# Sorting edges while a transformer runs: three tiles counted at once, in four parts of the edges, at two fixed places of a group

## The chip, the core and the metric

The kernel runs on one core of a Trainium2 chip. A core has a matrix engine (TensorE, PE in the rows; PEld is its weight load), a vector engine (VectorE, DVE), a scalar engine (ScalarE, ACT), a general-purpose engine (GpSimd, POOL) and a queue engine (SyncE, SP). Each runs its own instruction stream, and they wait for each other by semaphores. SP, ACT and POOL issue DMAs. The time is the device time of one launch in microseconds (us), lower is better; before and after are compared by the median of several runs.

## The reference

There are 6250 nodes with 256 features, and 100,000 edges with a source, a destination and a weight. Cut to what matters:

```python
xn = layernorm(x)
# gnn: edge attention, 4 heads of 64
feats = einsum('nd,hdo->hno', xn, Ws) + bs
a_s, a_d = feats . aw_src, feats . aw_dst
w = exp(-relu((a_s[src] + a_d[dst] + aw_e * edge_weight + ab) / 20))
gnn = segment_sum(w * feats[dst], src) / segment_sum(w, src)
# mix: 4 layers, 8 heads of 32, linear attention over all nodes
for l in range(4):
    h = layernorm(y) * g1 + b1
    q = softmax(h Wq * s, over a head's 32 columns)
    k = softmax(h Wk * s, over the 6250 nodes)
    y = y + (q (k^T (h Wv))) Wo + bo
    y = y + gelu((layernorm(y) * g2 + b2) W1 + c1) W2 + c2
x1 = x + gnn + mix
# ffn: 8 heads of 64 slices, attention among slices, weights over all nodes
x1 = x1 + slice_attention(layernorm(x1))
```

The edges come in no order of their source, so the sum over a node's edges needs them sorted by tiles of 125 source nodes.

## The kernel before, in words

The nodes are 50 tiles of 125 rows, and four tiles make a group: 13 groups, 0 to 12, the last with two tiles. All matrix work is fp32.

**One list orders all engines.** A planner writes `stages`, a list of steps with an assumed duration each: `x_t` (transpose the input rows), `feats` (edge features), `h1_t`, `keys`, `queries`, `q_exp`, `q_sum`, `q_norm`, `q_t` (the queries' softmax and its transpose), `ek_t`, `context` (transposed exponentials of the keys, and their product with h), `attend`, `h2_t`, `up`, `down` (the feed-forward half). Every engine walks the same list and issues its own share of each step, so the list is the program order of all of them. Three kinds of other work are laid into it at planned times, from a second list, `beside`, and a third, `blocks`:

- **The sort** (`sort`, L1069 and on), wholly on DVE. The edges lie as 125 rows of 800 columns. Steps 1 to 4 make each edge's tile number. Steps 5 to 29 (`FIRST_COUNT` on) count two tiles each: a match against the pair's number (L1101), a running sum along the row in which the odd tile has a weight of 2^10 (L1102), the row's total (L1103), the match times the sum (L1104), added to `rank` (L1105). One step is five instructions. Step 30 unpacks the two fields, and step 33 (`COUNT_STEP`) turns the totals into offsets with two matmuls of PE. Then four parts of 200 columns follow, 13 steps each; one of these steps looks up the offset of four tiles for the part (L1143 and L1144 for each tile). When a part is done, POOL scatters its 200 columns as records of 12 bytes to DRAM, one indirect DMA a column (L806), 800 in all.
- **The load of the sorted records** (`edges` on SP, `records` on DVE, `rows` on PE), at a planned time after the first part: 1.55 us for each column.
- **The edge blocks**, 220, spread evenly over the feed-forward groups from the records to the end of the last layer. For each, POOL gathers 4 x 128 rows of `gather_table` with four indirect DMAs (L772); DVE makes one-hot matrices, scores and weighted rows and adds the result into `acc` (L1158 to L1174, L1412); PE sums with twelve matmuls (L1746, L1757). A gather may run six blocks ahead, since it has a ring of six buffers.

**The first pass** is the stretch in which `x_t` and `feats` of group s stand beside layer 0's `context` of group s - 2 and `keys` and `queries` of group s - 1. Its sort steps stand 12 us of the plan apart, wherever that falls. After it come the last groups of a layer (`last_groups`, `finish`) and then the feed-forward groups of layer 0, which also hold the keys and queries of layer 1, and so on for four layers. The slice attention of `ffn` ends the kernel.

## Time and profile before

| | |
|---|---|
| runs | 3549.72, 3547.07, 3549.95 us; median 3549.72 |
| the profiled execution | 3542.55 us, its span 3540.8 us |
| busy in the span | PE 93%, DVE 66%, POOL 56%, ACT 34% |
| mean granted TensorE clock | 0.968 of 2.4 GHz |
| first pass | to 323 us |
| scatter of the records (L806) | 530 to 1788 us |
| gathers (L772) | 1811 to 3088 us |

All stretches below are microseconds from the span's start. Busy shares are averages over stages whose limits differ: PE is full where nothing else is laid in, and has gaps in the first pass, in the feed-forward groups that hold the sort, and in those that hold the edge blocks. The mean clock is below 1 where PE has had gaps.

### The profile page before, as it was taken

To read this page: it belongs to the slowest core of one execution; us is meant where nothing else is said; L and a number is where in the kernel's file an instruction comes from. 1 tells how busy PE (TensorE), PEld (TensorE's weight loads), DVE (VectorE), ACT (ScalarE), POOL (GpSimd) and SP (SyncE) were. 2 spreads that over 40 slices of the span, in tenths; PEclk is the share of its full clock that TensorE was granted. 3 is DMA by queue.
4 is the path that set the end of the run, shared out by engine and by line. 5 is a ranking of instruction groups with operands and counts; after the bars stand their busy time and mean duration, and the time that the engine had idled before them with its cause. 6 is when DMAs were issued, how large, how long until landed. Compare 5 with 4: busy or idle time off the path is not lost.

```text
span 3540.8 us, 43968 instructions
## 1 busy us (share of the span) xinstructions
PE 3280.0 (93%) x13948; PEld 2325.2 (66%) x13948; DVE 2344.0 (66%) x6105; ACT 1188.5 (34%) x2126; POOL 1981.9 (56%) x1746
## 2 busy tenths in 40 slices
PE   6887899999989999989999989988999999989989
PEld 4565566666756666766766666666766666655666
DVE  7887878885444444453468777776776767759941
ACT  3343232333333333333324433343433434312220
POOL 3210007777777777777746777774777777600000
PEclk9998999999999999999999999999999999999999
DMA  3332112222322222232234555554555555412124
GB/s 114 105 99 87 32 45 43 43 49 38 75 52 45 46 49 49 43 85 42 48 107 134 148 141 143 137 149 147 154 161 150 159 142 168 130 52 87 67 108 152
DMA packets 226436, 338.52 MB, mean 96 GB/s; under 512 B 52502, under 2 KB 180009, under 8 KB 225956
## 3 DMA queue, kind: packets, MB, share of 16 engines
q0 software_dynamic: 67840, 119.33, 15.7%
q1 hardware_dynamic: 120452, 161.93, 14.1%
q10 hardware_dynamic: 37920, 54.45, 4.8%
q8 instruction: 119, 1.95, 0.2%
q14 instruction: 105, 0.86, 0.1%
HBM read 247.40 MB, written 87.29 MB: 95 GB/s over the span
## 4 chain that ended last, share of the span: by engine, by line
PE 61%; DVE 13%; POOL 13%; issue 5%; DMA 4%; ACT 2%; DVEq 0%; ACTq 0%
PE bank_v L1715 14%; PE bank_a L1700 14%; POOL arena L772 13%; PE bank_e L1757 5%; PE bank_a L1617 4%; PE bank_v L1645 3%; PE bank_v L1605 3%; PE bank_v L1688 3%; PE bank_a L1546 3%; PE bank_v L1776 3%; DMA arena<-gather_table,arena 3%; PE bank_v L1866 3%; PE bank_v L1788 2%; PE bank_a L1628 1%; DVE acc L1102 1%
## 5 line engine op out<-in xcount | busy, mean ns | idle before, releaser
L806 POOL DMA_INDIRECT edge_records<-acc x800 | 962.7, 1203 | 535.3 <-issue 535.3
L772 POOL DMA_INDIRECT arena<-gather_table,arena x880 | 943.9, 1073 | 356.5 <-issue 260.2
L1715 PE MATMUL bank_v<-W_sb,gT 128*125 128x256 f32 x3200 | 746.7, 385 | 0.0
L1700 PE MATMUL bank_a<-hT,W_sb 128*128 128x500 f32 (+1 forms) x1664 | 716.6, 579 | 17.2 <-ACT gT L832 8.6
L1715 PEld LDWEIGHTS bank_v<-W_sb,gT 128*125 128x125 f32 x3200 | 592.3, 190 | 106.3 <-issue 23.2
L1700 PEld LDWEIGHTS bank_a<-hT,W_sb 128*128 128x128 f32 x1664 | 319.4, 195 | 327.6 <-issue 301.3
L1757 PE MATMUL bank_e<-arena 128*125 128x260 f32 x1760 | 454.9, 403 | 0.0
L832 ACT ACTIVATE gT<-bank_a,cols 128x500 f32<-128x500 f32 (+1 forms) x416 | 272.3, 661 | 377.4 <-PE bank_a L1700 376.5
L1757 PEld LDWEIGHTS bank_e<-arena 128*125 128x125 f32 x1760 | 322.1, 193 | 46.7 <-issue 1.4
L832 ACT ACTIVATE hT<-bank_a,cols 128x500 f32<-128x500 f32 (+1 forms) x208 | 144.9, 747 | 489.5 <-PE bank_a L1546 460.4
L1158 DVE TENSOR_TENSOR arena<-arena 128x1024 f32<-128x1024 f32 x220 | 268.2, 1219 | 0.0
L1351 DVE TENSOR_TENSOR xs<-bank_v,xs 125x512 f32<-125x512 f32 x100 | 68.8, 688 | 261.5 <-PE bank_v L1715 261.3
L966 ACT ACTIVATE esc<-esc 128x16 f32<-128x16 f32 x220 | 47.1, 214 | 554.9 <-DVE esc L1174 554.5
L1412 DVE TENSOR_TENSOR acc<-acc,bank_e 125x260 f32 x440 | 184.5, 419 | 65.0 <-PE bank_e L1757 44.7
L1263 DVE TENSOR_REDUCE kst<-bank_a 128x1 f32<-128x500 f32 (+1 forms) x104 | 67.1, 656 | 233.5 <-PE bank_a L1617 232.9
L1645 PE MATMUL bank_v<-h,ek 125*128 125x256 f32 x800 | 185.8, 385 | 3.1 <-ACT ek L832 3.1
L766 POOL TENSOR_SCALAR xs<-xs,st_x 125x256 f32<-125x256 f32 x50 | 68.7, 1383 | 213.2 <-DVE st_x L1042 213.2
L1617 PE MATMUL bank_a<-hT,Wqkv 128*128 128x500 f32 (+1 forms) x416 | 179.8, 574 | 8.9 <-ACT hT L832 8.9
L1605 PE MATMUL bank_v<-Wqkv,hT 128*125 128x256 f32 x800 | 183.8, 382 | 0.0
L1605 PEld LDWEIGHTS bank_v<-Wqkv,hT 128*125 128x125 f32 x800 | 151.7, 190 | 38.5 <-issue 17.7
L1645 PEld LDWEIGHTS bank_v<-h,ek 125*128 125x128 f32 x800 | 152.9, 193 | 25.7 <-DVE gT L1283 2.8
L832 ACT ACT_TABLE_LOAD x126 | 161.7, 1283 | 10.9 <-issue 5.0
(286 smaller groups left out, 4342.4 us busy)
## 6 DMA issues: line engine op xcount, KB each, us to landing
residual<-xs SPq DMA_DIRECT2D x60, 500.0 KB
xs<-residual SPq DMA_DIRECT2D x60, 500.0 KB
arena<-edge_rows ACTq DMA_DIRECT2D x220, 125.0 KB
queries<-qT_out SPq DMA_DIRECT2D x48, 500.0 KB
qT_in<-queries ACTq DMA_DIRECT2D x39, 500.0 KB
arena<-gather_table,arena POOLq DMA_INDIRECT x880, 3.7
edge_records<-acc POOLq DMA_INDIRECT x800
slice_weights<-arena SPq DMA_DIRECT2D x12, 1000.0 KB, 5.0
```

The costliest lines, as they stand in the source:

```text
L772: e.indirect_dma_start(g_of(j)[:, i, :], None, table_d, bass.IndirectOffsetOnAxis(ap=node[:, TE * j + i:TE * j + i + 1].bitcast(I32), axis ...
L806: e.indirect_dma_start(rec_d, bass.IndirectOffsetOnAxis(ap=pos_i[:, f:f + 1], axis=0), r3[:, f, :], None).then_inc(d_rec, 16)
L832: e.activation(to, of, func, **k).then_inc(a_done, 1)
L1158: e.tensor_tensor(gf, gf, bc(g[:, :, HG * DG:ROW].unsqueeze(3), [P, TE, HG, DG]), ALU.mult)\
L1412: e.tensor_tensor(to, to, ps_sum[h], ALU.add).then_inc(e_done[h], 1)
L1546: o = e.transpose(b[:, i * R:(i + 1) * R], X[:, i, c * P:(c + 1) * P], ident[0:R, 0:R])
L1605: o = e.matmul(b[0:R, i % 2 * D:(i % 2 + 1) * D], hv[:, k, i * R:(i + 1) * R], W[:, k, 0:D], start=k == 0, stop=k == KC - 1)
L1617: o = e.matmul(b[:, 0:n], W[:, k, D + c * P:D + (c + 1) * P], hv[:, k, 0:n], start=k == 0, stop=k == KC - 1)
L1645: o = e.matmul(b[:, c * D:(c + 1) * D], ek[:, a:a + P], h1[:, i * D:(i + 1) * D], start=i == 0, stop=i == tiles(s) - 1)
L1700: o = e.matmul(b[:, 0:n], W[:, k, f * P:(f + 1) * P], hv[:, k, 0:n], start=k == 0, stop=k == KC - 1)
L1715: o = e.matmul(b[0:R, i % 2 * D:(i % 2 + 1) * D], gv[:, f, i * R:(i + 1) * R], W2_sb[:, f * D:(f + 1) * D], start=False, stop=f == FB - 1 ...
L1757: o = e.matmul(ps_sum[h], oh_ring[j % NO][:, i * R:(i + 1) * R], g_of(j)[:, i, :], start=i == TH * h, stop=i == TH * (h + 1) - 1)
```

## The change

The sort counts three tiles in one step. A tile's number b is split into b // 3 and b % 3; the three kinds weigh 1, 256 and 65536 in the running sum. For a field to hold below 256, the sum starts anew in each of the four parts of 200 columns, so L1102 becomes four instructions over 200 columns in place of one over 800, and the totals are four columns a step. There are 17 such steps (4 to 20) in place of 25. Three steps (21 to 23) then unpack a field each, in place of one step, and step 23 adds the four parts' totals. `COUNT_STEP` is 25 in place of 33, and its offsets are made for each part (three more small additions). The preparation is rewritten (steps 1 to 3). The parts' 52 steps are as they were, but use their own part's offsets.

The plan changes too. In each group of the first pass the sort has two fixed places: after `context`, and between `queries` and `feats`. `feats` now stands in front of the queries' `q_exp`, `q_sum` and `q_norm`, and `q_t` moves from before `context` to after `h1_t`. After the first pass the rules are as before. Since there are eight steps fewer of 8 us, everything planned from the end of the first part moves: `edges` from 1651.65 to 1563.64 us of the plan, from the middle of group 4's `down` steps in layer 2 to group 2's, and the 220 blocks are spread over some two groups more: 3.35 us of the plan apart in place of 2.97, which is 13 or 14 blocks in a group of layer 2 in place of 15 or 16, and 9 or 10 in a group of layer 3 in place of 10 or 11.

```diff
-    FIRST_COUNT = 5
-    COUNT_STEP = FIRST_COUNT + NT // 2 + 3
+    FIRST_COUNT, NTRIO = 4, -(-NT // 3)
+    COUNT_STEP = FIRST_COUNT + NTRIO + 4
...
+    slots = []
     for s in range(2, NGR):
         put(1.05, "x_t", s)
         turn("ek_t", 0, s - 2)
+        context(0, s - 2)
+        slots.append(now())
+        turn("h1_t", 0, s - 1)
         turn("q_t", 0, s - 2)
-        context(0, s - 2)
-        turn("h1_t", 0, s - 1)
         keys(0, s - 1)
         if s <= PRE:
             queries(0, s - 1)
+        slots.append(now())
+        put(1.15 * tiles(s), "feats", s)
+        if s <= PRE:
             put(0.0, "q_exp", 0, s - 1)
             put(0.0, "q_sum", 0, s - 1)
             put(0.0, "q_norm", 0, s - 1)
-        put(1.15 * tiles(s), "feats", s)
...
     for k in range(SORT_STEPS):
+        if 1 <= k <= len(slots):
+            at = slots[k - 1] - 0.01
         beside.append((at, ("sort", k)))
-        at += 7.0 if k < FIRST_COUNT - 1 else 12.0 if at < mixed else 8.0 if k < COUNT_STEP else 4.5 if k < first_part else 7.0
+        at += 8.0 if k < COUNT_STEP else 4.5 if k < first_part else 7.0
...
-                elif FIRST_COUNT <= k < FIRST_COUNT + NPAIR:
+                elif FIRST_COUNT <= k < FIRST_COUNT + NTRIO:
                     b = k - FIRST_COUNT
-                    step(e.scalar_tensor_tensor(oh, pair, float(b), weight, ALU.is_equal, ALU.mult))
-                    step(e.tensor_tensor_scan(cum, oh, oh, 0.0, ALU.add, ALU.bypass))
-                    e.tensor_copy(cnt2[:, b:b + 1], cum[:, EC - 1:EC])
-                    step(e.scalar_tensor_tensor(oh, pair, float(b), cum, ALU.is_equal, ALU.mult))
+                    step(e.scalar_tensor_tensor(oh, trio, float(b), weight, ALU.is_equal, ALU.mult))
+                    for q in range(PARTS):
+                        o = e.tensor_tensor_scan(by_part(cum)[:, q, :], by_part(oh)[:, q, :], by_part(oh)[:, q, :], 0.0,
+                                                 ALU.add, ALU.bypass)
+                    step(o)
+                    e.tensor_copy(cnt3.rearrange("p (q b) -> p q b", q=PARTS)[:, :, b], by_part(cum)[:, :, PART - 1])
+                    step(e.scalar_tensor_tensor(oh, trio, float(b), cum, ALU.is_equal, ALU.mult))
                     step(e.tensor_tensor(rank, rank, oh, ALU.add))
...
+                elif FIRST_COUNT + NTRIO <= k < FIRST_COUNT + NTRIO + 3:
+                    m = k - FIRST_COUNT - NTRIO
+                    c3 = cnts.rearrange("p (q b k) -> p q b k", q=PARTS, k=3)[:, :, :, m]
+                    ci = trios[:, 0:PARTS * NTRIO]
+                    if m == 0:
+                        step(e.tensor_copy(pos_i, rank))
+                    step(e.tensor_copy(ci, cnt3))
+                    for a in (field, pos_i), (ci, ci):
+                        o = e.tensor_scalar(*a, 8 * m, 255, ALU.logical_shift_right, ALU.bitwise_and)
+                    step(o)
+                    e.tensor_copy(c3, ci.rearrange("p (q b) -> p q b", q=PARTS))
+                    if m == 0:
+                        step(e.scalar_tensor_tensor(rank, mod, 0.0, field, ALU.is_equal, ALU.mult))
+                    else:
+                        step(e.scalar_tensor_tensor(oh, mod, float(m), field, ALU.is_equal, ALU.mult))
+                        step(e.tensor_tensor(rank, rank, oh, ALU.add))
...
                     for b in range(4 * at, min(4 * at + 4, NT)):
-                        step(e.tensor_scalar(oh[:, h], bucket[:, h], float(b), adj[:, b:b + 1], ALU.is_equal, ALU.mult))
+                        step(e.tensor_scalar(oh[:, h], bucket[:, h], float(b), adj[:, part * NT + b:part * NT + b + 1],
+                                             ALU.is_equal, ALU.mult))
```

**On ACT, one group of the first pass, before** (`hT` with `cols` is `h1_t`, the other `hT` is `x_t`; `ekT` the keys' exponentials; L907 is `q_exp`; `h` and `gT` are `feats`):

```order
L832 ACTIVATE qT_out<-bank_a 128x500 x2
L832 ACTIVATE hT<-bank_a,cols 128x500 x2
L913 ACTIVATE kst<-kst 128x2
L832 ACTIVATE ekT,kst<-bank_a,kst 128x500 x2
L907 ACTIVATE qn<-qn 125x1024
L879 ACTIVATE h_1<-xs,st_x 125x256 x4
L832 ACTIVATE gT<-bank_a 125x264 x4
```

The same place after (L842, L889, L917 and L923 are those lines now):

```order
L842 ACTIVATE hT<-bank_a,cols 128x500 x2
L842 ACTIVATE qT_out<-bank_a 128x500 x2
L923 ACTIVATE kst<-kst 128x2
L842 ACTIVATE ekT,kst<-bank_a,kst 128x500 x2
L889 ACTIVATE h_1<-xs,st_x 125x256 x4
L842 ACTIVATE gT<-bank_a 125x264 x4
L917 ACTIVATE qn<-qn 125x1024
```

`q_exp`, which waits for DVE, has moved behind the features' evictions, and the eviction of `q_t` behind that of `h1_t`.

**On DVE, layer 1's queries of group 2, in a feed-forward group, before** (L1283 ends `queries`, L1335 is `attend`, L1292 and L1293 are `q_sum`, L1298 is `q_norm`; L1143 and L1144 are a sort step):

```order
L1292 TENSOR_REDUCE qst<-qn 125x32
L1293 RECIPROCAL qst<-qst 125x32
L1143 TENSOR_SCALAR acc<-acc 125x200
L1144 TENSOR_TENSOR acc<-acc 125x200
L1143 TENSOR_SCALAR acc<-acc 125x200
L1144 TENSOR_TENSOR acc<-acc 125x200
L1143 TENSOR_SCALAR acc<-acc 125x200
L1144 TENSOR_TENSOR acc<-acc 125x200
L1143 TENSOR_SCALAR acc<-acc 125x200
L1144 TENSOR_TENSOR acc<-acc 125x200
L1335 TENSOR_TENSOR xs<-bank_v,xs 125x512
L1298 TENSOR_TENSOR qn<-qn,qst 125x1024
```

The same queries after (L1308 and L1309, L1361, L1318, L1319, L1324; the sort step's lines are L1168 and L1170):

```order
L1309 TENSOR_TENSOR qn<-bank_v,qst 125x512
L1168 TENSOR_SCALAR acc<-acc 125x200
L1170 TENSOR_TENSOR acc<-acc 125x200
L1168 TENSOR_SCALAR acc<-acc 125x200
L1170 TENSOR_TENSOR acc<-acc 125x200
L1168 TENSOR_SCALAR acc<-acc 125x200
L1170 TENSOR_TENSOR acc<-acc 125x200
L1168 TENSOR_SCALAR acc<-acc 125x200
L1170 TENSOR_TENSOR acc<-acc 125x200
L1361 TENSOR_TENSOR xs<-bank_v,xs 125x512
L1318 TENSOR_REDUCE qst<-qn 125x32
L1319 RECIPROCAL qst<-qst 125x32
```

A sort step that stood between `q_sum` and `q_norm` now stands between `queries` and `q_sum`; in other groups the steps fall elsewhere.

**On PE, one edge block and what is around it in a group of layer 2, before** (L1746 and L1757 are the block's matmuls, L1761 its next row numbers; L1617 is `keys`, L1605 `queries`):

```order
L1617 MATMUL bank_a<-hT,Wqkv 128x500 x2
L1746 ISA
L1746 MATMUL bank_e<-as,arena 128x12 x2
L1746 ISA
L1746 MATMUL bank_e<-as,arena 128x12 x2
L1757 MATMUL bank_e<-arena 125x260 x4
L1761 TENSOR_LOAD tids
L1761 ISA x2
L1761 TENSOR_LOAD tids
L1761 ISA x2
L1617 MATMUL bank_a<-hT,Wqkv 128x500 x2
L1605 MATMUL bank_v<-Wqkv,hT 125x256 x4
```

And after (L1772, L1783, L1787; `keys` is L1643, `queries` L1631):

```order
L1643 MATMUL bank_a<-hT,Wqkv 128x500 x4
L1772 ISA
L1772 MATMUL bank_e<-as,arena 128x12 x2
L1772 ISA
L1772 MATMUL bank_e<-as,arena 128x12 x2
L1783 MATMUL bank_e<-arena 125x260 x4
L1787 TENSOR_LOAD tids
L1787 ISA x2
L1787 TENSOR_LOAD tids
L1787 ISA x2
L1631 MATMUL bank_v<-Wqkv,hT 125x256 x8
```

A block costs the same; more of the layer's own matmuls stand between two of them.

## Rows read from the trace of the kernel before

**Rows 1.** The page: busy time, then tenths busy in 40 slices.

```profile
PE 3280.0 (93%) x13948; PEld 2325.2 (66%) x13948; DVE 2344.0 (66%) x6105; ACT 1188.5 (34%) x2126; POOL 1981.9 (56%) x1746
...
DVE  7887878885444444453468777776776767759941
...
POOL 3210007777777777777746777774777777600000
PEclk9998999999999999999999999999999999999999
```

**Rows 2.** The page: the chain that ended last, by line.

```profile
PE bank_v L1715 14%; PE bank_a L1700 14%; POOL arena L772 13%; PE bank_e L1757 5%; PE bank_a L1617 4%; PE bank_v L1645 3%; PE bank_v L1605 3%; PE bank_v L1688 3%; PE bank_a L1546 3%; PE bank_v L1776 3%; DMA arena<-gather_table,arena 3%; PE bank_v L1866 3%; PE bank_v L1788 2%; PE bank_a L1628 1%; DVE acc L1102 1%
```

**Rows 3.** Groups by line, POOL, 1880 to 2380: busy, mean ns | idle before.

```profile
L772 POOL DMA_INDIRECT arena<-gather_table,arena x360 | 390.7, 1085 | 109.7 <-issue 107.5 <-PE bank_e L1757 2.1
```

**Rows 4.** The same, 2500 to 3080.

```profile
L772 POOL DMA_INDIRECT arena<-gather_table,arena x422 | 451.4, 1070 | 128.6 <-issue 125.2 <-PE bank_e L1757 3.4
```

**Rows 5.** Line L772: ns min/median/max, first and last start; who waited for it.

```profile
L772 POOL DMA_INDIRECT arena<-gather_table,arena x880: 940/946/2005, 1810.7 to 3087.1; - x176
...
  DVE esc L1174: 165.4, 84
```

**Rows 6.** Windows: us, then PE, PEld, DVE, ACT, POOL busy, granted clock, DMA.

```profile
106.85:304.98 198.13, 170.48 (x738) 122.74 (x737) 166.09 (x375) 80.65 (x176) 41.93 (x31) 0.91 0.29 93
...
431.91:875.89 443.98, 422.93 (x1679) 295.65 (x1678) 348.69 (x1027) 139.46 (x217) 263.71 (x220) 0.98 0.20 43
483.99:536.86 52.87, 48.49 (x187) 34.11 (x188) 46.76 (x145) 15.55 (x24) 5.45 (x5) 0.94 0.13 39
588.32:634.39 46.07, 45.88 (x187) 32.02 (x186) 41.63 (x122) 15.44 (x25) 35.14 (x30) 1.00 0.22 47
830.22:875.89 45.67, 45.67 (x187) 32.10 (x186) 21.67 (x65) 15.45 (x25) 34.72 (x30) 1.00 0.21 42
1900.00:2330.00 430.00, 396.81 (x1876) 291.60 (x1874) 338.33 (x875) 164.78 (x321) 335.99 (x309) 0.97 0.53 143
2490.00:3080.00 590.00, 555.28 (x2522) 399.25 (x2522) 414.71 (x1030) 237.93 (x416) 459.13 (x429) 0.98 0.55 154
```

**Rows 7.** Groups by line, DVE, 106.85 to 304.98: the counting steps.

```profile
L1102 DVE TENSOR_TENSOR_SCAN acc<-acc 125x800 f32<-125x800 f32 x14 | 27.2, 1944 | 0.5
L1101 DVE SCALAR_TENSOR_TENSOR acc<-acc 125x800 f32<-125x800 f32 x14 | 14.6, 1044 | 0.0
L1105 DVE TENSOR_TENSOR acc<-acc 125x800 f32<-125x800 f32 x14 | 14.4, 1026 | 0.5
L1104 DVE SCALAR_TENSOR_TENSOR acc<-acc 125x800 f32<-125x800 f32 x14 | 14.3, 1022 | 0.0
```

**Rows 8.** The same, DVE, 466 to 560: an instruction over 200 columns.

```profile
L1144 DVE TENSOR_TENSOR acc<-acc 125x200 f32<-125x200 f32 x65 | 23.9, 368 | 2.2
```

**Rows 9.** Pieces of the chain that ended last, after the first pass.

```profile
342.45 0.91 DVE acc L1101
```

**Rows 10.** Waits of PE, 431.91 to 875.89: us in total, times, longest.

```profile
PE bank_a L1546 <- DVE qn L1298: 19.1, 8, 4.4
```

**Rows 11.** Line L806, the scatter: ns min/median/max, first and last start.

```profile
L806 POOL DMA_INDIRECT edge_records<-acc x800: 1182/1187/2182, 530.2 to 1786.4; - x160
```

**Rows 12.** Timeline of SP, 1785 to 1792: start us, us.

```profile
1788.72 0.34 SPq L657 DMA_DIRECT2D queries<-qT_out  x1
1789.12 0.42 SPq L671 DMA_DIRECT2D arena<-edge_records  x1
```

**Rows 13.** Timeline of POOL, from 1865, and from 2415.

```profile
1871.05 0.97 POOL L772 DMA_INDIRECT arena<-gather_table,arena  x1 [18.62 <-PE bank_e L1757]
...
2451.68 0.94 POOL L772 DMA_INDIRECT arena<-gather_table,arena  x1 [35.30 <-PE bank_e L1757]
```

**Rows 14.** Timeline of PE, 1867 to 1875: a block and what follows.

```profile
1868.67 0.25 PE L1746 MATMUL bank_e<-as,arena 128*128 x4
...
1870.61 3.52 PE L1700 MATMUL bank_a<-hT,W_sb 128*128 128x500 f32 x8
```

87 lines of the change are left out of this document (41 added, 46 removed).

## The prediction, as put down before the run

> **What bounds the kernel now.** I read the page first. PE is busy for 93% of the span, and the rows of tenths say where it is not: DVE is nearly full in the first ten slices, POOL sits at a flat 7 tenths from slice 21 to 35, and PE's granted clock is 0.9 in the first four slices [rows 1]. The chain that ended last is mostly PE, but its third line is a POOL line, the gather L772, with 13% of the span [rows 2]. So I asked POOL's groups by line for the stretches with edge blocks. From 1880 to 2380, 360 gathers took 390.7 us and stood 109.7 us idle, 107.5 of it issue and only 2.1 waiting for PE: POOL does nothing but start one gather after another, one each 1.390 us [rows 3]. From 2500 to 3080 it is one each 1.374 us, 3.4 us of waiting in 580 [rows 4]. Seven tenths is POOL full. DVE waited for gathers 84 times, 165.4 us in all [rows 5]. In the same stretches PE lacks 33 of 430 us and 35 of 590, at clocks of 0.97 and 0.98 [rows 6]. I conclude that from about 1871 to 3088 POOL sets the pace, not PE, by its 880 gathers. When they may begin then matters more than what the sort costs.
>
> Earlier, the limits differ. In the first pass a group takes 198.13 / 8 = 24.77 us and DVE is busy for 84% of it. In the feed-forward groups that hold sort steps PE is the engine and loses time in single blows: a group without sort is 45.67 us, one that holds it well 46.07, one that holds it badly 52.87 at a clock of 0.94 [rows 6]. The blow is PE waiting for `q_norm`, 8 times for 19.1 us [rows 10].
>
> **Term 1, the first pass.** In the eight groups 4 to 11 DVE is busy for 166.09 us [rows 6]. 14 counting steps are in them, 27.2 + 14.6 + 14.4 + 14.3 = 70.5 us, 5.04 a step [rows 7]. The rest is 95.6 us, 11.9 a group, and idle time is 32.0 us, 4.0 a group. Now every group holds two counting steps. No row shows a scan over 200 columns. An instruction over 200 columns takes 368 ns and its like over 800 takes 1026 [rows 7, 8], which leaves a fixed part of (4 x 368 - 1026) / 3 = 149 ns. Four scans for one cost nothing more at best, if the fixed parts overlap (they have no wait between them), and 3 x 149 = 0.45 us more at worst. I take 0.35, near the upper end, since the nearest row is at it. A step is then 5.39 us, two 10.8, a group 22.7 us if DVE never idles and 26.7 if all of today's idle time stays. With `feats` in front of `q_exp`, ACT no longer makes PE's features wait for DVE's queries, and `q_norm` has a group's length until `q_t`; what should stay of the 4.0 us are the short gaps between dependent instructions, so I take 24.0. Eight groups give 8 x (24.0 - 24.77) = -6 us, between -16 and +16. PE then waits some 3 us a group for the keys' exponentials behind the first sort step: late next is ACT's `ekT`, released by DVE. The last group of the pass holds two unpacking steps in place of one counting step; it has no input statistics and no queries, so I put it at 0.
>
> **Term 2, between the first pass and the feed-forward.** Three counting steps stood there, of which the one that begins at 342.45 is on the chain that ended last [rows 9]. In their places stand now the third unpacking step (two instructions over 800 columns at about 1.03, one on integers no dearer, and some seven small ones: 3.9 us against 5.0) and an empty step (0 against 5.0). The step after them and the next are traded for `COUNT_STEP` and two lookups of eight 200-wide instructions, 8 x 0.37 = 2.9 us each, which I call even within 3 us. Sum -6 us.
>
> **Term 3, the sort in the feed-forward groups.** From 431.91 to 875.89 there are nine groups, 443.98 us [rows 6]. By the program's order five of them have a sort step between `q_sum` and `q_norm`, or the long unpacking step in front of `q_sum`; three have steps only where `q_exp` or the keys cover them; one has none. With 45.67 and 46.2 for the latter kinds the five come to (443.98 - 45.67 - 138.6) / 5 = 51.9 each, which is the 52.87 of the row. After, steps 46 and 66 fall between `q_sum` and `q_norm`, four groups have covered steps and three are empty: 2 x 51.9 + 4 x 46.2 + 3 x 45.67 = 425.6, so -18 us, between -8 (four blows) and -24 (one). What DVE saves in busy time, about 40 us, is not counted again: it is what these three terms are made of. Terms 1 to 3 are -30 us up to 876.
>
> **Term 4, the edges.** Today SP issues the load of the records at 1789.12, 0.4 us after the store of `queries` in front of it in the list [rows 12], and the last scatter starts at 1786.4 [rows 11]: place and readiness coincide. The place moves two feed-forward groups forward, 2 x 45.67 = 91, and with the 30 us comes at 1788.7 - 121 = 1668. Readiness: the first part now ends with step 38, in front of DVE's keys of the group whose `ek_t` is at 431.91 today; those begin some 8 us before it, so with 12 us gained and the step's own 3 the scatter starts near 415 in place of 530.2, and at today's length of 1256 us ends near 1672. SP waits about 5 us. Behind it on SP stands only the store of a group that DVE finishes later; behind that wait on DVE are the records' copies, some 20 us on. The first gather starts at 1810.7 today and near 1695 then. The ring of six first fills, and POOL is full from the fifth block on: 1871.05 today [rows 13], then 1871 - 91 + 8 (the block stands four and a half `up` steps further on, 1.76 each [rows 14]) - 30 = 1758. From there to the last gather it is 3087.1 - 1871 = 1216 us [rows 5, 13], the 35.3 us at the change of layers included; the gathers are the same, so the end comes 113 us earlier. Is PE in time? It lacked 68 us of 1020, and the clock's 0.97 and 0.98 cost 13 + 12, in all some 105 over 1216; the layer work that now lies within adds 83. PE needs 1216 - 105 + 83 = 1194 us. By the group of layer 2: 45.67 + 13.6 blocks x 1.94 [rows 14] = 72.1 for PE, 13.6 x 4 x 1.39 = 75.6 for POOL, in place of 76 and 87. Both are near full, so I take off 5 us for rubbing: -108 at the end of the blocks. Terms 1 to 3 are inside this, since they move the start. The rest of the kernel, from 3101 on, is the same work.
>
> A gather's median is 946 ns and its mean 1085 or 1070 [rows 3 to 5], so something stretches some of them. By the Trainium skill (SBUF — State Buffer, Who interferes with whom), copies and tensor_scalars of VectorE in a two-port mode hold a port pair shared with GpSimd, and the other engine is blocked for the whole instruction. If all the stretching came from the layer's own DVE work, 15.6 x 4 x 0.139 = 8.7 us a group would fall on 13.6 blocks: 0.02 us more a gather, 18 us in all, and the time would be 3460; if it came from the blocks' work, nothing.
>
> **Sum.** The profiled execution is 3542.55 us, its span 3540.8; 108 less is 3434.5. The runs' median is 3549.72, 7 us above it, and the time is compared with that: 3549.7 - 108 = 3442.
>
> **The rivals.**
> - *The first pass keeps its idle time.* A counting step after `context` meets POOL's normalisation, PE waits, its clock falls, and a group takes 27 us: 8 x (27 - 24.0) = +24, which moves the end one for one: 3466. For it: 26.7 is the bound above, and the clock there is 0.91 [rows 6]. Against it: PE has 3 us of slack a group. 14%.
> - *The blocks' losses are not POOL's.* If PE's gaps stay with the blocks for another reason, spreading them gives nothing, and only terms 1 to 3 remain: 3520. Against it: the 2.1 and 3.4 us of POOL's waits [rows 3, 4]. 8%.
> - *Slower: the edge stretch costs by the group, not by the block.* If a group of layer 2 with 13.6 blocks takes the 87 us that one with 15.6 takes, two more groups cost 2 x (87 - 45.67) = +83, less 30: 3602. It decides if DVE, 79% busy there (338.33 of 430 [rows 6]), sets the group rather than POOL. Against it: with two blocks fewer DVE has less to do. 4%.
> - *It doesn't start earlier.* If the scatter ends where it does today, the records wait for it, POOL's 1216 us begin at 1871 as now, and all of terms 1 to 3 is waited away: 3550. Against it: nothing stands between the first part and the scatter but a semaphore. 4%.
>
> **How the numbers follow.** The forecast, 3442, has 70%; its own range is 3424 to 3465. The range for 8 in 10 takes in the first rival and the ends of the unknown prices: 3415 to 3488; left out are the other rivals and a little of each tail. This kernel's measurement can tell about 0.2%, 7 us. Faster by more than that: 70 + 14 + 8 = 92%; within it 3% and slower 5%, from the last two.
>
> **What would show it.** The gather's first start near 1695 and its last near 2975, still one each 1.37 to 1.40 us with almost no wait for PE. The scatter's first start near 415, last near 1671. The windows of groups 4 to 11 at 24 us with DVE over 93% busy, and PE waiting for `ekT`. Waits of PE for `q_norm` in the feed-forward groups down from five of 3 to 4 us to two. Scans of 200 columns that start 0.43 to 0.59 us apart. The forecast is wrong if gathers wait for PE in long stretches (then PE is the bound), or if the first start of L772 has not moved by over 100 us.

## The result and the profile after

The changed kernel takes 3428.99 us, median of 4 runs (3426.59 to 3436.74), against 3549.10 (3547.07 to 3549.95; one run more than in the table above) of the kernel before on the same chip: ratio 0.9666, 95% interval 0.9649 to 0.9683, 120 us faster. The forecast was 3442. The profiled execution took 3427.19 us with a span of 3425.4. Lines of the code moved with the change: the gather is now L782 (was L772), the scatter L816 (was L806), the queries' softmax L1324 (was L1298).

The page, as [rows 1], and the chain that ended last, as [rows 2]:

```profile
PE 3236.0 (94%) x13948; PEld 2296.2 (67%) x13948; DVE 2302.2 (67%) x6124; ACT 1182.8 (35%) x2124; POOL 1980.3 (58%) x1746
...
DVE  7898888854544444544578878887677667659941
...
POOL 3210177777777777777557777775777777400000
PEclk9999999999999999999999999999999999989999
...
PE bank_a L1726 16%; PE bank_v L1741 15%; POOL arena L782 14%; PE bank_e L1783 6%; PE bank_a L1643 3%; PE bank_v L1671 3%; PE bank_v L1631 3%; PE bank_v L1802 3%; PE bank_v L1714 3%; PE bank_a L1572 3%; PE bank_v L1892 3%; PE bank_v L1814 2%; DVE acc L1110 1%; ACT arena L842 1%; DMA arena<-gather_table,arena 1%
```

POOL's row, idle for three slices behind the first pass before, is at 0 for one and at 1 for the next: the scatter starts sooner. At its far end the gathers stop in the same slice as before, which is 122 us earlier, since a slice is 85.6 us here and was 88.5. They are still on the chain, with 14%.

Windows (us, busy of PE, PEld, DVE, ACT, POOL, granted clock, DMA), as [rows 6]: first-pass groups 4 to 11; nine feed-forward groups; one with step 46 in front of `q_norm`; one with covered steps; one with step 66 in front of `q_norm`; one without sort; then two stretches of edge blocks.

```profile
109.29:296.19 186.90, 162.07 (x737) 114.71 (x737) 177.69 (x432) 78.51 (x176) 39.47 (x31) 0.99 0.31 99
411.97:836.95 424.98, 415.42 (x1676) 290.47 (x1674) 306.64 (x898) 139.25 (x217) 327.05 (x271) 0.99 0.22 45
458.52:507.63 49.11, 46.12 (x187) 32.08 (x186) 40.99 (x119) 15.53 (x25) 37.43 (x32) 1.00 0.23 44
554.10:600.71 46.61, 45.88 (x188) 32.00 (x186) 39.01 (x117) 15.38 (x24) 33.96 (x29) 1.00 0.22 46
600.71:653.40 52.69, 48.77 (x188) 34.20 (x187) 41.93 (x118) 15.64 (x25) 42.04 (x35) 0.94 0.21 41
791.28:836.95 45.67, 45.67 (x188) 32.09 (x186) 21.46 (x65) 15.46 (x25) 35.69 (x30) 1.00 0.21 42
1790.00:2200.00 410.00, 398.10 (x1905) 294.53 (x1905) 333.64 (x879) 172.37 (x324) 320.10 (x296) 0.99 0.54 148
2370.00:2960.00 590.00, 572.99 (x2628) 413.68 (x2627) 418.90 (x1060) 248.55 (x430) 432.86 (x404) 1.00 0.54 154
```

A first-pass group now takes 186.90 / 8 = 23.36 us with DVE busy for 95%. The nine feed-forward groups take 424.98, 19 less. In the edge stretch PE lacks 12 of 410 and 17 of 590, where it lacked 33 of 430 and 35 of 590.

The counting steps of the first pass by line, as [rows 7] (the sum is now four of 200 columns):

```profile
L1110 DVE TENSOR_TENSOR_SCAN acc<-acc 125x200 f32<-125x200 f32 x63 | 34.0, 599 | 0.6
L1108 DVE SCALAR_TENSOR_TENSOR acc<-acc 125x800 f32<-125x800 f32 x16 | 17.0, 1060 | 0.0
L1115 DVE TENSOR_TENSOR acc<-acc 125x800 f32<-125x800 f32 x15 | 14.9, 991 | 0.5
L1114 DVE SCALAR_TENSOR_TENSOR acc<-acc 125x800 f32<-125x800 f32 x15 | 14.7, 983 | 0.0
```

The gathers by line, 1760 to 2260 (answers to [rows 3]) and 2380 to 2960 (to [rows 4]):

```profile
L782 POOL DMA_INDIRECT arena<-gather_table,arena x361 | 389.5, 1079 | 111.6 <-issue 107.3 <-PE bank_e L1783 4.3
...
L782 POOL DMA_INDIRECT arena<-gather_table,arena x403 | 432.6, 1073 | 157.1 <-issue 118.1 <-PE bank_e L1783 39.0
```

The gather's line as a whole, with its first and last start and who waited for it (to [rows 5]), then the scatter's (to [rows 11]):

```profile
L782 POOL DMA_INDIRECT arena<-gather_table,arena x880: 940/947/2003, 1682.6 to 2965.3; - x176
...
  DVE esc L1200: 82.0, 48
```

```profile
L816 POOL DMA_INDIRECT edge_records<-acc x800: 1182/1187/2215, 408.7 to 1667.2; - x160
```

A gather each 1.388 us in the first window, as before. Of the 39.0 us of waiting in the second, 31.8 are the change of layers, which lies in it. DVE's own wait for gathers has halved.

The timelines of POOL (as [rows 13]) and of SP (as [rows 12]):

```profile
1750.22 0.94 POOL L782 DMA_INDIRECT arena<-gather_table,arena  x1 [26.87 <-PE bank_e L1783]
...
2402.05 0.94 POOL L782 DMA_INDIRECT arena<-gather_table,arena  x1 [31.80 <-PE bank_e L1783]
```

```profile
1660.53 0.35 SPq L667 DMA_DIRECT2D queries<-qT_out  x1
1670.70 0.34 SPq L681 DMA_DIRECT2D arena<-edge_records  x1
```

The fifth block, from which POOL is full, resumes at 1750.22 in place of 1871.05. From there to the last gather it is 2965.3 - 1750.2 = 1215.1 us, against 1216.

### The profile page after: what moved, and what is told of

It is laid out like the page before. It is cut to its first block, busy times and chain, and to the rows that moved or that the text cites. A ratio compares the mean times of both kernels' runs of the same rounds, so it can differ in the third digit from the quotient of the medians.

```text
span 3425.4 us, 43999 instructions
## 1 busy us (share of the span) xinstructions
PE 3236.0 (94%) x13948; PEld 2296.2 (67%) x13948; DVE 2302.2 (67%) x6124; ACT 1182.8 (35%) x2124; POOL 1980.3 (58%) x1746
## 4 chain that ended last, share of the span: by engine, by line
PE 64%; POOL 14%; DVE 12%; issue 5%; DMA 2%; ACT 2%; DVEq 0%; ACTq 0%
PE bank_a L1726 16%; PE bank_v L1741 15%; POOL arena L782 14%; PE bank_e L1783 6%; PE bank_a L1643 3%; PE bank_v L1671 3%; PE bank_v L1631 3%; PE bank_v L1802 3%; PE bank_v L1714 3%; PE bank_a L1572 3%; PE bank_v L1892 3%; PE bank_v L1814 2%; DVE acc L1110 1%; ACT arena L842 1%; DMA arena<-gather_table,arena 1%
## 5 line engine op out<-in xcount | busy, mean ns | idle before, releaser
L816 POOL DMA_INDIRECT edge_records<-acc x800 | 963.5, 1204 | 419.8 <-issue 419.8
L782 POOL DMA_INDIRECT arena<-gather_table,arena x880 | 942.4, 1071 | 355.6 <-issue 259.2
L1783 PE MATMUL bank_e<-arena 128*125 128x260 f32 x1760 | 442.0, 394 | 0.0
L842 ACT ACTIVATE gT<-bank_a,cols 128x500 f32<-128x500 f32 (+1 forms) x416 | 273.3, 661 | 408.9 <-PE bank_a L1726 408.0
L1783 PEld LDWEIGHTS bank_e<-arena 128*125 128x125 f32 x1760 | 314.4, 188 | 43.6 <-issue 1.4
L842 ACT ACTIVATE hT<-bank_a,cols 128x500 f32<-128x500 f32 (+1 forms) x208 | 144.9, 747 | 485.5 <-PE bank_a L1572 468.3
L1184 DVE TENSOR_TENSOR arena<-arena 128x1024 f32<-128x1024 f32 x220 | 267.9, 1218 | 0.0
L1643 PE MATMUL bank_a<-hT,Wqkv 128*128 128x500 f32 (+1 forms) x416 | 180.2, 574 | 6.2 <-ACT qT_out L842 4.0
L1631 PE MATMUL bank_v<-Wqkv,hT 128*125 128x256 f32 x800 | 181.9, 379 | 0.0
L1631 PEld LDWEIGHTS bank_v<-Wqkv,hT 128*125 128x125 f32 x800 | 150.0, 188 | 38.8 <-issue 18.5
```

The source lines that it names most:

```text
L782: e.indirect_dma_start(g_of(j)[:, i, :], None, table_d, bass.IndirectOffsetOnAxis(ap=node[:, TE * j + i:TE * j + i + 1].bitcast(I32), axis ...
L816: e.indirect_dma_start(rec_d, bass.IndirectOffsetOnAxis(ap=pos_i[:, f:f + 1], axis=0), r3[:, f, :], None).then_inc(d_rec, 16)
L842: e.activation(to, of, func, **k).then_inc(a_done, 1)
L1184: e.tensor_tensor(gf, gf, bc(g[:, :, HG * DG:ROW].unsqueeze(3), [P, TE, HG, DG]), ALU.mult)\
L1631: o = e.matmul(b[0:R, i % 2 * D:(i % 2 + 1) * D], hv[:, k, i * R:(i + 1) * R], W[:, k, 0:D], start=k == 0, stop=k == KC - 1)
L1643: o = e.matmul(b[:, 0:n], W[:, k, D + c * P:D + (c + 1) * P], hv[:, k, 0:n], start=k == 0, stop=k == KC - 1)
```

## The experiments

Milestones read from the profiles, in us. "Mark" is the start of the keys' transposition (`ek_t`) that ends the nine feed-forward groups, 875.89 before [rows 6]. "Fifth" is the start of the gather with which the fifth block resumes. Ratios are to the kernel before on the same chip. `e8`, `e10` and `e11` ran in a job in which the kernel before itself took 3661 us; in its three profiles the edge stretch alone is longer, so of these three only ratios and what lies before 1757 are compared with the others.

| kernel | first-pass group | mark | scatter | first gather | fifth | last gather | gather, mean ns | ratio |
|---|---|---|---|---|---|---|---|---|
| before | 24.77 | 875.89 | 530.2 to 1786.4 | 1810.7 | 1871.05 | 3087.1 | 1073 | 1 |
| changed | 23.36 | 836.95 | 408.7 to 1667.2 | 1682.6 | 1750.22 | 2965.3 | 1071 | 0.9666 |
| e1 edges late | 23.58 | 838.92 | 408.1 to 1666.3 | 1773.0 | 1833.24 | 3051.0 | 1075 | 0.9903 |
| e2 count only | 23.70 | 865.50 | 457.2 to 1716.2 | 1742.9 | 1808.89 | 3044.7 | 1098 | 0.9867 |
| e3 order only | 23.07 | 855.98 | 494.3 to 1754.3 | 1767.2 | 1832.92 | 3063.1 | 1092 | 0.9921 |
| e4 features behind | 23.55 | 840.92 | 413.1 to 1680.0 | 1690.9 | 1754.15 | 2980.4 | 1085 | 0.9668 |
| e5 half multiply | 23.83 | 839.46 | 411.1 to 1677.8 | 1688.5 | 1751.84 | 2930.7 | 1010 | 0.9585 |
| e6 no blows | 23.74 | 829.88 | 411.0 to 1676.1 | 1687.1 | 1744.78 | 2970.9 | 1083 | 0.9641 |
| e7 and sooner | 23.53 | 829.23 | 401.2 to 1656.5 | 1668.5 | 1728.22 | 2944.1 | 1075 | 0.9614 |
| e9 old places | 23.91 | 867.54 | 460.6 to 1729.1 | 1744.5 | 1810.84 | 3041.3 | 1087 | 0.9867 |
| e8 masked sum | 23.55 | 839.49 | 409.8 to 1669.2 | 1684.6 | 1757.84 | (3075.9) | 1084 | 0.9679 |
| e10 edges sooner | 23.74 | 832.03 | 404.7 to 1660.1 | 1670.9 | 1733.00 | (3063.1) | 1082 | 0.9633 |
| e11 denser steps | 23.57 | 837.46 | 397.5 to 1659.5 | 1669.9 | 1731.08 | (3049.0) | 1080 | 0.9627 |
| e12 shifted steps | 23.96 | 870.12 | 524.6 to 1780.8 | 1805.1 | 1865.42 | 3082.1 | 1072 | 0.9982 |

**e1: the edges late.**

```
-    edges_at = sorted_part + 1.55 * EC
+    edges_at = sorted_part + 1.55 * EC + 88.0
```

> The changed kernel, with the records' load and the edge blocks put back to where the kernel before had them in the program (88 us of the planner's time later); the sort is untouched. Theory (POOL's chain of gathers sets the end): the gathers start later by the two feed-forward groups, last gather near 1832 + 1216 = 3048, time 3512 us (3500 to 3520), 83 us above the changed kernel; SP does not wait for the scatter. Rival (the blocks' losses are not POOL's, the gain is all from the shorter sort): no change against the changed kernel, 3429. Rival (the edge stretch costs by the group): fewer groups hold blocks, so it is faster than 3429, near 3350.

Measured: 3508.90 us (3504.10 to 3516.16), ratio 0.9903, 95% interval 0.9883 to 0.9923. The gathers by line, first and last start:

```profile
L782 POOL DMA_INDIRECT arena<-gather_table,arena x880: 942/947/2005, 1773.0 to 3051.0; - x176
```

The fifth block is 83.0 us later than in the changed kernel, the last gather 85.7 (3048 was forecast), the time 80 by the medians and 84 by the ratios (83 was). The two rivals, 3429 and 3350, are out. This is the largest part of the gain: the shorter sort alone, with the edges where they were, gives 34 us by the ratio, 37 by the medians.

**e2 and e3: each half alone.** The first takes the counting of three tiles and leaves the old order and places, so against the changed kernel it has the edit below and the first pass's loop of the kernel before; the second takes the new loop and the two fixed places (the edit the other way round, on the kernel before) and leaves the counting of two tiles.

```
-        if 1 <= k <= len(slots):
-            at = slots[k - 1] - 0.01
         beside.append((at, ("sort", k)))
-        at += 8.0 if k < COUNT_STEP else 4.5 if k < first_part else 7.0
+        at += 7.0 if k < FIRST_COUNT - 1 else 12.0 if at < mixed else 8.0 if k < COUNT_STEP else ...
```

> The changed kernel with three tiles counted at once, but with the first pass in the order of the kernel before and the sort steps in the old places (one each 12 us of planned time); with fewer steps the edges stand 59 us of planned time earlier than before, 29 later than in the changed kernel. Theory: first-pass groups stay near 25 us, four blows of the sort in the feed-forward groups, so about 14 us gained up to 837 in place of 38.9, and 61 from the earlier gathers: 3549 - 75 = 3474 us (3464 to 3486). Rival (the earlier gathers bring nothing, only the shorter sort does): 3549 - 14 = 3535. Rival (the order of the first pass and its two places bring nothing): 3429.

> The kernel before (two tiles counted at once, one scan of 800 columns) with the new order of the first pass and its two places for steps. 22 of the steps stand in the places; the edges stand 24 us of planned time earlier than before. Theory: first-pass groups of 22.7 to 23.4 us, so 12 us; four blows in place of five, 5 us; earlier gathers 25 us: 3549 - 42 = 3507 us (3496 to 3516). If the two halves add up, the losses of this and of the kernel that only counts otherwise are 42 + 75 = 117 of 120. Rival (the first pass gained by the cheaper counting and not by its order): first-pass groups near 24.8, 3519.

Measured: e2 3498.67 us (3494.41 to 3503.13), ratio 0.9867 (0.9849 to 0.9886); e3 3519.52 (3509.62 to 3525.22), ratio 0.9921 (0.9899 to 0.9944). At the mark they had gained 10.4 and 19.9 us (14 and 17 were forecast), together less than the 38.9 of the changed kernel. But both ended later than forecast, by 25 and 12 us, and outside their ranges. e3's 3519.52 is the figure of its rival, but not for the rival's reason: its first-pass groups took 23.07 us and not 24.8. 10 of e2's are an error of the forecast: it took all of the two groups for the place, where the changed kernel itself gets some 83. The rest lies between the fifth block and the last gather, 1235.8 and 1230.2 us in place of 1215 to 1218, with this page row of e2 beside that of the changed kernel:

```profile
L776 POOL DMA_INDIRECT arena<-gather_table,arena x880 | 966.1, 1098 | 362.4 <-issue 259.6
```

```profile
L782 POOL DMA_INDIRECT arena<-gather_table,arena x880 | 942.4, 1071 | 355.6 <-issue 259.2
```

880 x 0.027 = 24 us more in gathers that were longer on the mean. So the halves, some 47 and 28 us by their ratios, do not add up to the whole gain: 9 us are missing at the mark and some 35 in longer gathers (why they were longer stands under e5). Over all ordinary runs but e5 the length of the stretch follows the mean gather: 1215 to 1218 us at 1071 to 1075 ns, 1226 at 1083 and 1085, 1230 at 1087 and 1092, 1236 at 1098. The idle time between gathers barely moves with it. This is what a chain set by POOL looks like.

**e4: the features put back behind the softmax.**

```
-        put(1.15 * tiles(s), "feats", s)
         if s <= PRE:
             put(0.0, "q_exp", 0, s - 1)
             ...
+        put(1.15 * tiles(s), "feats", s)
```

> The changed kernel with only the features put back behind the queries' softmax (feats after q_exp, q_sum, q_norm in the first pass). Theory: PE's features wait for ACT's exponential again, which waits for DVE's queries behind a sort step, and a first-pass group takes about 1 us more than 23.36: 10 groups, 3439 us (3433 to 3447), clock in these groups under 0.99. Rival (DVE, 95% busy, hides the order): 3429, groups of 23.4.

Measured: 3430.48 us (3425.04 to 3437.21), ratio 0.9668 (0.9653 to 0.9684): no difference. PE's waits in the eight groups, of e4:

```profile
PE bank_a L1622 <- ACT gT L842: 13.3, 8, 2.1
```

and of the changed kernel:

```profile
PE bank_a L1622 <- ACT ekT L842: 14.3, 8, 2.3
```

In both it is the features' matmuls that wait for ACT, 1.7 and 1.8 us a group: in e4 for the eviction of features before them (`gT`), in the changed kernel for the keys' exponentials (`ekT`). DVE is busy for 96% and 95% of these groups, and the order only chooses for which of ACT's outputs PE stands. The rival holds.

**e9 and e12: the places.** e9 is the changed kernel, its new order too, with the old places; e12 the kernel before with steps 5 to 19 shifted by 5 us into the places that they have in e2.

```
 e12: -        beside.append((at, ("sort", k)))
      +        beside.append((at + (5.0 if 5 <= k and at + 5.0 < mixed else 0.0), ("sort", k)))
```

> The changed kernel with the new order of the first pass (context first, q_t behind h1_t, features in front of the softmax) but the sort steps in the old places, one each 12 us of planned time. It differs from the kernel that only counts otherwise by the order alone, and from the changed kernel by the places alone. Theory (the order brings nothing, as moving the features back brought nothing; the fixed places bring the gain of the first pass and the fewer blows): first-pass groups near 23.7, 10 us gained up to 837, 3498 (3490 to 3505). Rival (the order brings the gain): first-pass groups of 23.0 to 23.3, 20 us or more gained up to 837, 3488 or less.

> The kernel before (two tiles at once, one sum over 800, old order) with only steps 5 to 19 of the sort 5 us of planned time later in the first pass, so that they stand in exactly the places in which the kernel that only counts otherwise has them; from step 20 on the order is that of before. Theory (where a step falls among the keys, the context and the softmax decides, not the counting): first-pass groups fall from 24.77 to 23.7 as there, 8 us come out by 305 and stay as the place of the records' load moves with them: ratio 0.9976 to the kernel before, 3540. Rival (the counting of three tiles with its shorter instructions did it): groups stay at 24.8, ratio 1.000.

Measured: e9 3498.23 us (3495.65 to 3503.99), ratio 0.9867 (0.9849 to 0.9885), the same as e2: the order without the places brings nothing. The places bring 30.6 us at the mark: 4.5 before group 4, 4.4 in the eight groups, 6.1 up to the first feed-forward group, and 15.6 in the nine feed-forward groups, into which fewer steps are left to fall. e12 3538.93 us (3533.90 to 3543.54, 12 runs), ratio 0.9982 (0.9974 to 0.9991): 6 us gained by a shift of 5 us and nothing else, with groups of 23.96. Where the steps fall decides, then, and less so how they count. First-pass groups with identical code (the changed kernel, e1, e5, e6) lie between 23.36 and 23.83, so differences under half a microsecond are not told apart here; the 0.55 us between e9 and the changed kernel is hardly more.

**e8: one masked sum for four.**

```
-                    for q in range(PARTS):
-                        o = e.tensor_tensor_scan(by_part(cum)[:, q, :], by_part(oh)[:, q, :], ...)
-                    step(o)
+                    step(e.tensor_tensor_scan(cum, ew, oh, 0.0, ALU.mult, ALU.add))
 and once, in step 3:
+                    step(e.memset(ew, 1.0))
+                    e.memset(by_part(ew)[:, :, 0], 0.0)
```

> The changed kernel with one running sum over 800 columns that a mask sets back to nothing at the three part borders (state x mask + input), in place of four sums over 200. The result is the same. Theory (the fixed parts of the four overlap, one sum of 800 took 1944 ns before and four take 1.97 us, 2.39 beside POOL's normalising): 0 to 0.4 us a step, of which at most 0.3 comes out in the first pass where DVE is 95% busy: groups of 23.0 to 23.4, 3426 us (3420 to 3431). Rival (a sum with a product on the way takes twice as long): 2 us a step more in 17 steps, groups of 27, 3455 or more.

Measured: ratio 0.9679 (0.9666 to 0.9692), the same as the changed kernel within the intervals. The sums of the changed kernel beside no work of POOL, and beside its normalising:

```profile
130.24 1.97 DVE L1110 TENSOR_TENSOR_SCAN acc<-acc 125x200 f32<-125x200 f32 x4
...
143.73 2.39 DVE L1110 TENSOR_TENSOR_SCAN acc<-acc 125x200 f32<-125x200 f32 x4
```

and of e8:

```profile
129.70 1.82 DVE L1111 TENSOR_TENSOR_SCAN acc<-acc 125x800 f32<-125x800 f32 x1
...
143.06 2.06 DVE L1111 TENSOR_TENSOR_SCAN acc<-acc 125x800 f32<-125x800 f32 x1
```

Four parts cost 0.15 and 0.33 us more than one, 0.24 on the mean of these two, where the prediction took 0.35 between 0 and 0.45. The other counting steps of both traces take these same times, and so does the single sum of the kernel before (1.82 and 2.06). It does not show in the time. The rival is out: the first-pass groups took 23.55 us, not 27. The forecast in us cannot be set beside this job's times.

**e5: half of DVE's multiply.**

```
+                gf, al = gf[:, 0:TE // 2], g[:, 0:TE // 2, HG * DG:ROW]
+                e.tensor_tensor(gf, gf, bc(al.unsqueeze(3), [P, TE // 2, HG, DG]), ALU.mult)
```

> The changed kernel in which the multiply of the gathered values by their weights (L1184, 128x1024 out of SBUF, 1.07 us) takes only the first two of the four tiles of a block; the weighting of the other two is left out. Over 1800 to 2100 a gather that overlaps with this multiply is longer: a fit of the gathers' lengths gives 0.94 us without overlap and 0.7 us for each us of overlap, 0.18 us a gather on the mean, half of which should go: mean of 1071 ns down to about 985. Theory (POOL and PE are both near full in the edge stretch): POOL needs 78 us less, but PE lacks only about 12 us of 410, 17 of 590 and some at the layers' change, so 20 to 25 us come out: 3407 (3398 to 3414), and POOL then waits for PE. Rival (POOL alone is the bound): 3429 - 78 = 3351. Rival (the stretching comes from elsewhere): mean gather stays at 1071, 3425 to 3429.

Measured: 3401.07 us (3395.66 to 3402.01), ratio 0.9585 (0.9568 to 0.9602), 28 us less than the changed kernel and inside the forecast range. The mean gather fell from 1071 to 1010 ns, 61 of the 86 forecast. Here are DVE and POOL of the changed kernel over the same 13 us (start, us):

```profile
1799.11 1.22 DVE L1184 TENSOR_TENSOR arena<-arena 128x1024 f32<-128x1024 f32 x1
...
1804.50 1.22 DVE L1184 TENSOR_TENSOR arena<-arena 128x1024 f32<-128x1024 f32 x1
```

```profile
1798.18 0.95 POOL L782 DMA_INDIRECT arena<-gather_table,arena  x1 [0.30 <-issue]
1799.43 1.71 POOL L782 DMA_INDIRECT arena<-gather_table,arena  x1 [0.30 <-issue]
1801.45 0.95 POOL L782 DMA_INDIRECT arena<-gather_table,arena  x1 [0.31 <-issue]
...
1803.96 0.94 POOL L782 DMA_INDIRECT arena<-gather_table,arena  x1 [0.30 <-issue]
1805.20 1.34 POOL L782 DMA_INDIRECT arena<-gather_table,arena  x1 [0.30 <-issue]
```

It is not the overlap as such that costs. The gather of 1803.96 was under way when the multiply began at 1804.50, and took 0.94. Those of 1799.43 and 1805.20 began while a multiply ran; they ended 0.81 and 0.82 us after the multiply's end. The whole trace of the changed kernel has the same two kinds. In 178 gathers the multiply began while they were under way: none took over 0.96 us. 217 began while it ran: they took 1.36 us on the mean and, but for two that began in its first tenth of a microsecond, none ended less than 0.81 us after it. These 217 hold 90 of the 111 us by which the 880 gathers exceed 0.945 us each.

This also answers why the gathers of e2 and e3 were longer. There, too, 220 gathers began inside the multiply, but at an earlier point of it, with 0.65 and 0.62 us of it still to run in place of 0.54 in the changed kernel, and they took 1.46 and 1.43 us. That is 22 of the 24 us that e2's gathers took more, and 16 of the 19 of e3's. What sets the point at which they begin was not varied. In e5 only 107 gathers began inside the halved multiply; the 90 us fell to 28, and 8 us came back beside other instructions.

POOL by the mean alone would have needed 850 x 0.061 = 52 us less for the stretch; 36 came out (1178.9 in place of 1215.1), since PE was then the limit: between the fifth block and the last gather POOL waited 65 times for PE, 101.2 us, in place of 28 times, 70.9 us. PE's windows in e5:

```profile
1790.00:2200.00 410.00, 406.19 (x1948) 299.63 (x1947) 304.99 (x896) 180.13 (x338) 309.33 (x308) 1.00 0.57 152
2370.00:2930.00 560.00, 554.88 (x2556) 402.62 (x2555) 360.97 (x1034) 242.97 (x416) 411.30 (x407) 1.00 0.57 160
```

PE lacks 4 of 410 and 5 of 560. So POOL was the bound in the changed kernel, and PE stands some 36 us behind it.

**e6 and e7: without the two blows, and the scatter sooner.**

```
+        held = item[0] in ("ek_t", "q_norm", "ln2") or item[0] == "attend" and item[3] > 0
         while beside and beside[0][0] <= at and (...)\
+                and not (held and beside[0][1][0] == "sort" and beside[0][1][1] > first_part):
 e7 as well:
-        at += 8.0 if k < COUNT_STEP else 4.5 if k < first_part else 7.0
+        at += 8.0 if k < COUNT_STEP else 3.5 if k < first_part else 7.0
```

> The changed kernel in which a sort step past the first part never stands in front of ek_t, the second attend, q_norm or ln2: steps 46 and 66 move behind ln2, nothing else. Theory: both waits of PE for the queries' softmax go, all groups take 46 us, 9 us gained up to 837. But the records are ready only when the last scatter ends, near 1667 as now, and the place of their load, on which SP waited 10 us already, only moves earlier: the first gather stays near 1682 and the end with it: 3427 (3421 to 3430). Rival (the end follows the start of the feed-forward groups): 3420.

> The same, and the steps up to the end of the first part one each 3.5 us of planned time in place of 4.5; the first scatter and the edges both move 13 us earlier. Theory: the scatter starts near 396 and ends near 1654, the first gather comes near 1669, 13 us earlier, and with PE near full in the edge stretch 8 to 13 us of it come out: 3418 (3412 to 3424). Rival (DVE, 79% busy between the first pass and the feed-forward groups, delays PE there by what the denser steps take): the scatter starts no earlier than 405, 3428.

Measured: e6 3420.63 us (3415.86 to 3428.06), ratio 0.9641 (0.9627 to 0.9655); e7 3407.64 (3402.06 to 3413.94), ratio 0.9614 (0.9600 to 0.9629). PE's waits for the queries' softmax from the first feed-forward group to the mark, of e6:

```profile
PE bank_a L1574 <- DVE qn L1326: 3.1, 5, 0.7
```

and of the changed kernel:

```profile
PE bank_a L1572 <- DVE qn L1324: 9.5, 6, 3.9
```

Both blows are gone, worth 9.3 us over the nine groups and 7 at the mark. The theory held that the records' readiness was already the limit and nothing would come out. The medians say 8 us, the ratios 9, but the intervals of the ratios just overlap, and the profiled execution of e6 (3428.06) is the slowest of its five and no faster than that of the changed kernel. So a gain is likely, its size not well known. The fifth block came 5.4 us earlier in e6 although the first gather came 4.5 later: between the first gather and the fifth block there were 67.6 us in the changed kernel and only 57.7 in e6. That interval had slack. e7, with a scatter that begins 7.5 us earlier (13 was forecast), had its fifth block 22.0 us earlier: 13 by the plan, most of the rest by the mark. Against the changed kernel it gained 21 us by the medians and 18 by the ratios, more than its forecast (8 to 13) or its rival (none); against e6, on the same chip, 13. It is the fastest of the whole kernels tried.

**e10 and e11: further.**

```
 e10, against e7: +    edges_at = sorted_part + 1.55 * EC - 12.0
 e11, against e7: +        at += 8.0 if k < COUNT_STEP else 2.6 if k < first_part else 7.0
```

> The kernel with no blows and steps of 3.5 us, with the records' load and the edge blocks alone another 12 us of planned time earlier; the scatter stays and ends near 1656. Theory (the blocks' places set when POOL becomes full, as the run without blows showed, as long as the first gathers are there): the first gather stays near 1668, the fifth block resumes near 1716 in place of 1728, and the end is 8 to 12 us earlier than 3407.6: 3398 (3394 to 3402). Rival (with this the scatter's end sets it): SP waits 20 us and more for the scatter, PE and DVE stand still for it, the fifth block stays near 1728 and the time near 3408 or above.

> The same places of the edges as in the run with the edges 12 us sooner, but reached by sort steps one each 2.6 us of planned time up to the end of the first part, so that the scatter also starts 12 us earlier (near 390). Theory (places and scatter move together): 12 us less than 3407.6: 3396 (3391 to 3401). Against the run before it, it tells what the scatter's end costs there. Rival (DVE cannot take a step each 2.6 us between the first pass and the feed-forward groups: PE waits for it): the first feed-forward group starts over 5 us later and the time is 3402 or more.

Measured, as ratios: e10 0.9633 (0.9620 to 0.9646), e11 0.9627 (0.9614 to 0.9640), neither better than e7, as far as ratios of that job can be set beside those of another. SP issued the records' load in e10 at

```profile
1663.03 0.35 SPq L683 DMA_DIRECT2D arena<-edge_records  x1
```

3 us behind the last scatter, and DVE stood 15.5 us for it (8.7 in e7). The fifth block came at 1733.0 and 1731.1, not at 1716: the rival holds for e10. In e11 the scatter began only 4 us earlier than in e7, and its first feed-forward group began at 421.4, where e7's did at 412.6: the rival holds there too, DVE has no room for a step each 2.6 us. A rule that was fitted afterwards, and not tested: the fifth block comes at the later of its place in the plan and some 60 us behind the first gather. Taking the place from the changed kernel (913 us behind the mark, less the shift of the edges in the plan), it gives those of e4, e5, e6, e7, e10 and e11 to within 3 us; that of e8 came 5 us later.

## Why the prediction was right, point by point

*What bounds.* "POOL sets the pace, not PE": shown, by e1 (place against time, 83 for 80 us), by the stretch's length following the mean gather, and by e5. The forecast for it, 1216 us from the fifth block on, measured 1215.1. The 5 us taken off for rubbing were not needed. The check on PE holds too: by the prediction's own rates PE lacks 93 of 1020 us, which is 111 and not 105 over 1216, so that it needs 1188; e5's 1178.9 is the length at which PE became the limit.

*Term 1*, -6 us, measured -11.2: groups of 23.36 where 24.0 was forecast, inside the bounds. The step's price, 5.39 us with 0.35 for the parts, was slightly high: e8 puts the parts at 0.24. What failed is the reason given for the lost idle time: the features in front of `q_exp` bring nothing (e4), nor does the order (e9 against e2); the places of the steps do (0.8 us a group in e12). So this term came out in the right direction partly by luck. "Late next is ACT's `ekT`" is right, 14.3 us in eight groups (3 us a group were forecast, 1.8 came). The clock there rose from 0.91 to 0.99, but the identical first pass of e5 ran at 0.93 with a group of 23.83, so up to half a microsecond a group of this gain is chance of one execution. The four sums of a step start 0.46 to 0.74 us apart, where 0.43 to 0.59 was expected. The last group of the pass, put at 0, brought 2.0 us, and the stretch before group 4 cost 2.4.

*Term 2*, -6, measured 108.73 - 99.57 = -9.2 between the transpositions that frame it (323.18 to 431.91 before, 312.40 to 411.97 after). *Term 3*, 425.6 us forecast, 424.98 measured; both blows stand where they were said to be, in the groups of steps 46 and 66, and PE's waits for the softmax there fell from 19.1 us in 8 [rows 10] to 9.5 in 6. At the mark 30 us were forecast and 38.9 came; this is the larger half of what was missing.

*Term 4.* The scatter starts at 408.7 (415 forecast) and ends near 1668 (1672), SP waits for it 10 us (5). The first gather starts at 1682.6 (1695), the fifth block at 1750.2 (1758), the last gather at 2965.3 (2975). The steps of the sum hold to within 13 us, most of that from terms 1 and 2.

*The sum.* The last gather starts 121.8 us earlier than before, where 113 were forecast ahead of the rubbing and 108 behind it; the missing 9 are those of the mark. All in all the profiled executions gained 7.4 us more than the 108: 8.8 at the mark and 5 of rubbing, less 6.4 behind the last gather. The other 5 of the 13 us between 3442 and 3429 are the distance of the medians from the profiled executions. The last block starts 3101.2 - 2982.0 = 119.2 earlier, but the span is only 115.4 shorter: "the rest of the kernel is the same work" is true of the work and not of its time. In both kernels PE waits 11 us for DVE's `xs` in this tail. The windows of the changed kernel in front of that wait, behind it, and a little later:

```profile
2982.00:3022.00 40.00, 39.10 (x172) 30.57 (x170) 16.03 (x49) 9.15 (x16) 0.00 (x0) 1.00 0.11 33
3036.00:3044.00 8.00, 8.00 (x9) 2.48 (x9) 4.65 (x7) 0.00 (x0) 0.00 (x0) 0.50 0.61 184
3048.50:3061.00 12.50, 12.50 (x15) 3.97 (x15) 7.09 (x7) 0.34 (x1) 0.00 (x0) 0.50 0.15 49
3061.35:3063.50 2.15, 2.15 (x6) 0.79 (x5) 1.38 (x2) 0.00 (x0) 0.00 (x0) 1.00 0.00 0
```

The clock is at the lower of its levels, 0.50 (1.2 GHz), for both stretches behind the wait. The timeline of PE of the kernel before has the same wait and one slow matmul group behind it (and one more, of 3.43 us, behind a second wait of 3 us):

```profile
3155.24 3.78 PE L1776 MATMUL bank_v<-Wqkv,hT 128*125 128x512 f32 x4 [11.11 <-DVE xs L1351]
3159.48 1.98 PE L1776 MATMUL bank_v<-Wqkv,hT 128*125 128x512 f32 x4
```

The medians differ by 120.1 and the profiled executions by 115.4: the one of before lies 6.6 us under its median, the one of after 1.8.

*The port rule weighed there* (the Trainium skill, SBUF — State Buffer, Who interferes with whom) would put the stretching down to VectorE's copies and tensor_scalars in a two-port mode. The trace shows another partner: the 128x1024 TENSOR_TENSOR with both inputs in SBUF, 1.71 us for a gather that begins inside it and 0.95 otherwise. Of the 111 us of stretching in the changed kernel 16 more belong to gathers that begin inside the one-hot's 128x500 TENSOR_TENSOR, and 3 to those inside a TENSOR_SCALAR. So the stretching comes from the blocks' own work, the case in which the prediction expected no loss. The same section names such an instruction as in the way of GpSimd's reads, but infers that descriptor generation is not among them; e5's 1071 to 1010 ns speaks against that inference. The 18 us that the rule's reading would have cost did not come in the changed kernel; e2 and e3 lost 24 and 19 us by longer gathers. The mean varies between 1071 and 1098 ns with the point of the multiply at which the gathers begin (under e5).

*The rivals.* The first pass kept no idle time; e5 and e1 exclude that the losses were not POOL's; the group was not the unit (e1); and the start did move.

*What stays open* besides what sets that point: in one job the kernel before took 3661 us, where it took 3545 in another on the same chip, and the changed ones were longer in proportion. In the profile of e8 the stretch from the fifth block to the last gather was 1318 us at a mean gather of 1084 ns, 80.4 us of POOL's idle time being put down to a releaser that the profile calls remote; e10 and e11, of the same job, have 78.2 and 82.1 us of it, and the profiles of the other jobs none. All that comes before 1757 and after the last gather was as usual. The cause is not known.

## What to carry to other kernels

When one engine starts one transfer after another without a pause, its start time is the quantity to work on: find what the first of them waits for (here a place in a hand-made order and the end of a scatter), and move the later of the two; when both coincide, moving one alone gives at most the slack between them. Price a stretch by its total length over the count, and watch the mean, not the median, of the bounding instruction: in e2 the median gather stayed at 946 ns while the mean moved by 27 and the stretch by 21 us. A step that runs beside a pipeline costs little or much by the place it falls in, a few microseconds either way, and an order on an engine that is not the bound only changes which wait is named.
